# Three products of 256 columns in place of each one-element filler on TensorE, in the partial first and last passes of a pipelined block

## The chip, the cores and the metric

The kernel runs on one NeuronCore of a Trainium2 chip. The metric is the device time of one execution in microseconds. The other engines named here are VectorE (DVE), ScalarE (ACT), GpSimd (POOL) and SyncE (SP), which issues the transfers. TensorE is PE, and its weight loads are shown as PEld.

## The reference

Two gated cross-attention and feed-forward layers over 64 batch rows, each of 256 tokens by 256 features, with a context of 120 tokens. Cut to what matters:

```python
x = x + tanh(g_xattn[0]) * L0_xattn(ctx, ctx, layernorm(x))    # 16 heads, softmax over the heads
x = x + tanh(g_ffn[0])   * L0_ffn(layernorm(x))                # silu(x Wg) * (x Wu) Wd, hidden 768
x = x + tanh(g_xattn[1]) * L1_xattn(layernorm(x), ctx)         # 16 heads that share one key and value
x = x + tanh(g_ffn[1])   * L1_ffn(layernorm(x))                # x (W + low rank).T + b
```

## The kernel before, in words

The four parts are the stages A, B, C and D of a software pipeline. Pass t runs stage A of batch row t - 2, stage B of the row before it, stage C of the row before that, and stage D (with the second half of C) of the row three behind; `live(t, behind)` says whether such a row exists. With 64 rows the passes run from t = 2 to t = 68. The passes 5 to 65 are a hardware loop in which every stage is live. The three passes ahead of it (2, 3, 4) and the three behind it (66, 67, 68) are written out and are partial.

On each engine the order of a pass is written out by hand in `one_pass`, and the engines wait for one another through semaphores that count passes. So that the counts stay right in a partial pass, an operation whose row does not exist is replaced by a filler which raises the same semaphore: on TensorE `skipped(bank)` at L1217, a product of one element by one element into the bank that the real operation would write; on DVE a memset of one element (L842), on ACT a copy of one element (L516), on POOL a memset of one element (L361). The wait in front of the operation stands ahead of the filler too.

Names that the prediction uses, by the semaphore that TensorE raises. Stage A: T_mm_A (transposes, L1120), k0_mm (keys, L1098), q_mm_A (queries, 12 products, L1081 to L1083), A0_mm and A1_mm (scores of a half of the tokens, L1173), A0_sub and A1_sub (subtract the maximum, L1189), v0_mm (L1104). Stage B: yA1_mm (attended values, L1203), woA_mm (14 products), T_mm_B, G_mm 0 to 5 (12 products each), dn_mm 0 to 5. Stage C: T_mm_C, kv1_mm, q_mm_C, M0_mm and M1_mm (L1162), mT_mm (L1196), T0_mm and T1_mm (L1183), zC1_mm, woC_mm. Stage D: T_mm_D and f1_mm (14 products). `ln_A` to `ln_D` are the layer norms that ACT applies (L475), after DVE's moments (L775 to L784) and POOL's root (L336 and L339).

A product in float32 is two instructions of TensorE, one in float32r (`w_hi`, `w_lo`, the `xt_`, `y_` and `h_` tiles) is one.

Of the kernel before, what the change touches and what calls it, by code (L numbers as in the profile page):

```python
# [29 lines left out]
B, S, SC, D = 64, 256, 120, 256  # L30
H, HD = 16, 16
HID = 768
P = 128
# [44 lines left out]
def flamingo_kernel(nc, xp, cp, wc, wf, wi, brow, gates, cst, ldT, da, luT, uaT, out):  # L78
# [3 lines left out]
    with ctx:  # L82
        def sb(name, shape, dt=F32):
            return ctx.enter_context(nc.sbuf_tensor(name, shape, dt))
# [5 lines left out]
        w_hi = sb("w_hi", [P, WCOLS], F32R)  # L90
        w_lo = sb("w_lo", [P, WCOLS], F32R)
        ident = sb("ident", [P, P])
# [11 lines left out]
        key_bias = sb("key_bias", [P, 2, KC])  # L104
        bias_row = sb("bias_row", [1, 2 * D])
        val_bias = sb("val_bias", [P, D])
        spare = {e: sb(f"spare_{e}", [1, 400]) for e in ("act", "dve", "pool")}
        minus_half = sb("minus_half", [P, NT])

        x_ln = sb("x_ln", [P, NT, D])  # L110
# [941 lines left out]
        def _(pe):  # L1052
# [3 lines left out]
            for i, name in enumerate(("q0", "k0")):  # L1056
                for x in range(KC):
# [3 lines left out]
                      start=True, stop=True).then_inc(s["bias_mm"], 1)  # L1061
# [4 lines left out]
            for kc in range(KC):  # L1066
                last = pe.matmul(W[2][:, kc * D:(kc + 1) * D], t2_s[:, kc * P:(kc + 1) * P], uaT_s[:, :],
                                 start=True, stop=True)
# [146 lines left out]
                                lambda r, par: e1[0:SC, cc, r, par, :], 0, S)  # L1215

            def skipped(bank):  # L1217
                return pe.matmul(bank[0:1, 0:1], ident[0:1, 0:1], ident[0:1, 0:1], start=True, stop=True, skip_group_check=True)

            def one_pass(t):  # L1220

                pe.wait_ge(s["res_D"], t - 1)
                if live(t, 2):
                    gate_up(W[0], 5).then_inc(s["G_mm"], 1)
                else:
                    skipped(W[0]).then_inc(s["G_mm"], 1)
                pe.wait_ge(s["max_rows"], 64 * (t - 1))
                pe.wait_ge(s["A1_exp"], nth(0, 2, t))
                if live(t, 3):
                    scores1(0).then_inc(s["T0_mm"], 1)  # L1230
                else:
                    skipped(scores[:, 0, :]).then_inc(s["T0_mm"], 1)
                pe.wait_ge(s["v0_pad"], t - 1)
                if live(t, 2):
                    down(W[2], 0).then_inc(s["dn_mm"], 1)
                else:
                    skipped(W[2]).then_inc(s["dn_mm"], 1)
# [235 lines left out]
```

## Time and profile before

| | |
|---|---|
| time, median of 3 | 2813.01 us (2812.63 to 2813.55) |
| the profiled execution's own time | 2812.17 us |
| its span | 2810.4 us |
| PE busy | 2656.1 us (95%) |
| DVE busy | 2469.6 us (88%) |
| ACT, POOL busy | 1563.9 us (56%), 1427.9 us (51%) |
| mean granted TensorE clock | 0.987 |
| first filler of TensorE | 46.3 us |
| last filler of TensorE | 2807.4 us |

Times in the rows are counted from the span's start. The row PEclk gives the clock that TensorE was granted, 1.00 (2.4 GHz) or 0.50 (1.2 GHz); a mean between the two is a stretch with a change in it. "Idle before" is the time in which an engine had nothing running ahead of the group, and the name after it is what ended the wait.

### The profile page before, as it was taken

Reading aid. Unit: us, or ns where it says so; the run is one execution under the profiler, and the core shown is the slowest. Engines: PE = TensorE matmul, PEld = TensorE weight load, DVE = VectorE, ACT = ScalarE, POOL = GpSimd, SP = SyncE. Lnnn points to the kernel's source line nnn. Section 1 sums busy time; section 2 is a strip of 40 time slices with the busy share of each in tenths; the row PEclk is TensorE's granted clock in tenths of the full one; section 3 lists DMA queues with packets and bytes.
Section 4 is the critical chain, followed back from the end, with each engine's and each line's share of the span. In section 5 each row is a group of like instructions: output and inputs, shape, how many; then the busy total and the mean of one; then the engine's idle time right before and its main releaser. Section 6 shows DMA issues by size and latency. Waiting matters only on the chain.

```text
span 2810.4 us, 75822 instructions
## 1 busy us (share of the span) xinstructions
PE 2656.1 (95%) x30576; PEld 2278.9 (81%) x30576; DVE 2469.6 (88%) x4425; ACT 1563.9 (56%) x3125; POOL 1427.9 (51%) x1591
## 2 busy tenths in 40 slices
PE   3799999999999999999999999999999999999996
PEld 2688888888888888888888888888888888888884
DVE  4589999999999999999999999999999999999973
ACT  3355555555555555555555555555555555555553
POOL 1454465465455455456456446546545545545630
PEclk9799999999999999999999999999999999999997
DMA  2000000000000000000000000000000000000000
GB/s 76 24 22 25 26 25 29 23 27 28 21 28 27 21 30 25 21 30 25 25 27 25 25 26 27 28 21 27 28 21 30 25 21 30 25 21 30 25 16 9
DMA packets 74668, 73.15 MB, mean 26 GB/s; under 512 B 6907, under 2 KB 73745, under 8 KB 74642
## 3 DMA queue, kind: packets, MB, share of 16 engines
q1 hardware_dynamic: 74642, 72.80, 8.5%
q8 instruction: 17, 0.28, 0.0%
q14 instruction: 9, 0.07, 0.0%
HBM read 54.94 MB, written 16.78 MB: 26 GB/s over the span
## 4 chain that ended last, share of the span: by engine, by line
PE 36%; DVE 25%; POOL 24%; issue 6%; ACT 3%; DMA 2%; SPq 2%; POOLq 1%; DVEq 0%
POOL zt L345 8%; PE work L1081 8%; POOL h_lo L342 8%; PE work L1203 7%; PE work L1083 6%; PE work L1082 6%; DVE m L821 5%; POOL zt L349 4%; PE scores L1173 3%; DVE x L836 3%; POOL zt L352 2%; DVE y1f L833 2%; DVE e L830 2%; ACT e L509 2%; DMA x_ln<-xp 2%
## 5 line engine op out<-in xcount | busy, mean ns | idle before, releaser
L509 ACT ACTIVATE e<-scores 120x1024 f32<-120x1024 f32 x512 | 504.6, 1024 | 178.7 <-PE scores L1183 163.8
L342 POOL TENSOR_TENSOR h_lo<-h_f,h_hi 128x256 fp32r<-128x256 f32 x384 | 401.9, 1061 | 192.4 <-ACT h_hi L468 192.4
L1081 PE MATMUL work<-xt_hi_B,w_hi 128*128 128x256 f32 x1536 | 442.4, 288 | 0.9 <-DVE h_f L811 0.5
L1082 PE MATMUL work<-xt_lo_B,w_hi 128*128 128x256 f32 x1536 | 429.4, 280 | 0.0
L1083 PE MATMUL work<-xt_hi_B,w_lo 128*128 128x256 f32 x1536 | 428.5, 279 | 0.0
L830 DVE TENSOR_TENSOR e<-e,rz 120x2048 f32<-120x2048 f32 x128 | 383.8, 2998 | 2.2
L345 POOL TENSOR_TENSOR zt<-e 120x512 f32<-120x512 f32 x256 | 332.0, 1307 | 57.4 <-ACT e L509 57.4
L817 DVE TENSOR_REDUCE m<-scores 120x128 fp32r<-120x2048 f32 x128 | 293.3, 2291 | 27.6 <-PE scores L1173 24.3
L1081 PEld LDWEIGHTS work<-xt_hi_B,w_hi 128*128 128x128 f32 x1536 | 289.1, 188 | 11.8 <-DVE h_f L811 0.7
L1082 PEld LDWEIGHTS work<-xt_lo_B,w_hi 128*128 128x128 f32 x1536 | 289.5, 188 | 2.9
L1083 PEld LDWEIGHTS work<-xt_hi_B,w_lo 128*128 128x128 f32 x1536 | 289.1, 188 | 0.0
L336 POOL TENSOR_TENSOR rstd_B<-var_eps_B,minus_half 128x2 f32<-128x2 f32 x64 | 67.2, 1050 | 425.0 <-DVE var_eps_B L784 425.0
L336 POOL TENSOR_TENSOR rstd_D<-var_eps_D,minus_half 128x2 f32<-128x2 f32 x64 | 44.1, 689 | 463.3 <-DVE var_eps_D L784 463.3
L821 DVE TENSOR_REDUCE m<-scores 128x16 f32<-128x1920 f32 x128 | 274.8, 2147 | 5.0 <-PE scores L1162 4.8
L1081 PE MATMUL work<-w_hi,h_hi 128*128 128x256 f32 x768 | 228.9, 298 | 30.1 <-POOL h_lo L342 30.1
L1203 PE MATMUL work<-e,v_pad 120*32 120x128 f32 (+1 forms) x6144 | 237.7, 311 | 1.1 <-DVE e L830 1.1
L468 ACT ACTIVATE h_hi<-h_f 128x256 fp32r<-128x256 f32 x384 | 148.0, 420 | 142.2 <-DVE h_f L811 142.1
L833 DVE RECIPROCAL y1f<-y1f 128x256 f32<-128x256 f32 x128 | 222.8, 1742 | 2.0 <-ACT y1f L568 2.0
L1203 PEld LDWEIGHTS work<-e,v_pad 120*32 120x32 f32 x6144 | 180.2, 111 | 45.8 <-DVE e L830 1.6
L1082 PE MATMUL work<-w_lo,h_hi 128*128 128x256 f32 x768 | 214.8, 280 | 0.0
L1083 PE MATMUL work<-w_hi,h_lo 128*128 128x256 f32 x768 | 214.8, 280 | 0.0
L1081 PEld LDWEIGHTS work<-w_hi,h_hi 128*128 128x128 f32 x768 | 144.3, 188 | 81.4 <-POOL h_lo L342 60.1
(192 smaller groups left out, 7323.1 us busy)
## 6 DMA issues: line engine op xcount, KB each, us to landing
x_ln<-xp SPq DMA_DIRECT2D x64, 256.0 KB, 2.7
x_res<-xp SPq DMA_DIRECT2D x64, 256.0 KB, 2.7
y<-y_out SPq DMA_DIRECT2D x64, 256.0 KB, 2.2
ctx_f_A<-cp SPq DMA_DIRECT2D x64, 128.0 KB, 2.5
ctx_f_C<-cp SPq DMA_DIRECT2D x64, 128.0 KB, 2.0
qm<-mT SPq DMA_DIRECT2D x256, 4.0 KB
e<-wi SPq DMA_DIRECT2D x3, 768.0 KB, 5.9
e<-wf SPq DMA_DIRECT2D x2, 512.0 KB, 3.6
```

The lines of the kernel that those rows point to most:

```text
L342: return pool.tensor_tensor(h_lo[:, m, :], h_f[:, m % 2, :], h_hi[:, m, :].bitcast(F32), ALU.subtract)
L345: return pool.tensor_tensor(zt[0:SC, c, 4 * h:4 * h + 4, :], e0[0:SC, c, 2 * h, :, :], e0[0:SC, c, 2 * h + 1, :, :], ALU.add)
L468: return act.activation(out, src, ACT.Copy)
L509: return act.activation(e[0:SC, c, 2 * h:2 * h + 2, :, :].rearrange("p a b n -> p (a b n)"), scores[0:SC, 2 * h:2 * h + 2, :].rearrange("p ...
L817: return dve.tensor_reduce(m0[0:SC, c, :], scores[0:SC, :, :].rearrange("p r (h n) -> p n (r h)", n=P), AX.X, ALU.max)
L821: return dve.tensor_reduce(m1[:, c, :].rearrange("p (r x) -> p r x", r=RG)[:, :, 0:4], scores[:, :, :].rearrange("p r (h n) -> p r h n", n ...
L830: return dve.tensor_tensor(e, e, rz0[0:SC, c:c + 1, :].to_broadcast([SC, H, P]), ALU.mult)
L833: return dve.reciprocal(y1f[:, cc * S:(cc + 1) * S], y1f[:, cc * S:(cc + 1) * S])
L1081: pe.matmul(out, a_hi, b_hi_, start=first, stop=False, skip_group_check=parts)
L1082: pe.matmul(out, a_hi, b_lo_, start=False, stop=False, skip_group_check=parts)
L1083: last = pe.matmul(out, a_lo, b_hi_, start=False, stop=end, skip_group_check=parts)
L1203: last = pe.matmul(bank[32 * r:32 * r + 32, cc * S + query:cc * S + query + n], v_of(4 * cc + r, par), e_of(r, par), start=par == 0, stop= ...
```

## The change

Each filler of TensorE becomes three products in float32r of 128 by 128 by 256: weights `w_hi[:, 0:128]`, moving data `w_hi[:, 0:256]`, written over the first 256 columns of the same bank on all its 128 partitions. Only the last raises the semaphore. The fillers of the other engines stay, and the spare tiles that they write are cut from 400 to 170 elements.

```diff
-        spare = {e: sb(f"spare_{e}", [1, 400]) for e in ("act", "dve", "pool")}
+        spare = {e: sb(f"spare_{e}", [1, 170]) for e in ("act", "dve", "pool")}
...
             def skipped(bank):
-                return pe.matmul(bank[0:1, 0:1], ident[0:1, 0:1], ident[0:1, 0:1], start=True, stop=True, skip_group_check=True)
+                for n in range(3):
+                    last = pe.matmul(bank[:, 0:S], w_hi[:, 0:P], w_hi[:, 0:S], start=True, stop=True, skip_group_check=True)
+                return last
```

TensorE at the start of pass 2, from its first filler to the keys of stage A; `work` is one of the four banks, `scores` the first bank of the scores:

```order
-L1218 MATMUL work<-ident 1x1
-L1218 MATMUL scores<-ident 1x1
-L1218 MATMUL work<-ident 1x1 x4
-L1218 MATMUL scores<-ident 1x1
-L1218 MATMUL work<-ident 1x1 x8
+L1219 MATMUL work<-w_hi 128x256 x3
+L1219 MATMUL scores<-w_hi 128x256 x3
+L1219 MATMUL work<-w_hi 128x256 x12
+L1219 MATMUL scores<-w_hi 128x256 x3
+L1219 MATMUL work<-w_hi 128x256 x24
 L1120 MATMUL work<-ident,xn_A 128x128 x4
 L1098 MATMUL work<-ctx_f_A,wk 128x128 x4
```

The same fifteen fillers stand in the same places, now as 45 products; nothing changes place.

TensorE in pass 68, the last, from the first scores of stage C to the last attended values:

```order
 L1183 MATMUL scores<-qm,km 128x256 x8
-L1218 MATMUL work<-ident 1x1 x4
+L1219 MATMUL work<-w_hi 128x256 x12
 L1183 MATMUL scores<-qm,km 128x256 x8
 L1203 MATMUL work<-e,ones_pad 32x256 x8
-L1218 MATMUL work<-ident 1x1 x2
+L1219 MATMUL work<-w_hi 128x256 x6
 L1203 MATMUL work<-e,ones_pad 32x256 x8
-L1218 MATMUL work<-ident 1x1
+L1219 MATMUL work<-w_hi 128x256 x3
 L1203 MATMUL work<-e,v_pad 32x256 x16
```

Twelve products stand between the two score groups instead of four one-element fillers, and six between the two sums over the keys.

## Rows read from the trace of the kernel before

**Rows 1.** The page: TensorE's share, and two rows of the 40 equal slices.

```profile
PE 2656.1 (95%) x30576; PEld 2278.9 (81%) x30576; DVE 2469.6 (88%) x4425; ACT 1563.9 (56%) x3125; POOL 1427.9 (51%) x1591
...
PE   3799999999999999999999999999999999999996
...
PEclk9799999999999999999999999999999999999997
```

**Rows 2.** Windows: stretch, length, PE, PEld, DVE, ACT, POOL busy, clock, DMA.

```profile
51.40:58.80 7.40, 6.13 (x36) 5.46 (x34) 1.69 (x11) 1.87 (x7) 0.18 (x2) 1.00 0.14 37
59.50:62.90 3.40, 1.34 (x36) 1.14 (x36) 1.88 (x2) 0.58 (x4) 0.00 (x0) 1.00 0.02 5
63.40:74.50 11.10, 8.80 (x56) 5.72 (x57) 5.86 (x12) 4.79 (x12) 6.04 (x9) 0.56 0.13 36
...
94.40:100.80 6.40, 6.17 (x30) 5.73 (x30) 1.43 (x6) 2.06 (x5) 0.09 (x1) 0.53 0.00 0
...
2749.20:2752.60 3.40, 1.72 (x15) 1.35 (x14) 3.18 (x6) 2.06 (x7) 0.00 (x0) 1.00 0.00 0
2752.60:2759.40 6.80, 5.79 (x38) 4.66 (x37) 2.80 (x6) 1.97 (x6) 0.09 (x1) 0.50 0.01 2
2761.40:2767.00 5.60, 0.61 (x14) 0.31 (x10) 3.43 (x11) 1.38 (x5) 0.89 (x2) 0.94 0.00 0
...
2801.00:2807.00 6.00, 4.65 (x27) 4.02 (x28) 0.94 (x7) 1.28 (x9) 0.35 (x4) 0.50 0.01 3
```

**Rows 3.** TensorE's fillers by form: count, ns min/median/max, first and last start.

```profile
L1218 PE MATMUL work<-ident x162: 158/158/160, 46.3 to 2807.4; 1*1 1x1 f32 x162
...
L1218 PE MATMUL scores<-ident x60: 158/158/160, 46.5 to 2807.1; 1*1 1x1 f32 x60
```

**Rows 4.** Timeline of passes 2 and 3: start, length, engine, line; pairs of successive products.

```profile
57.14 0.41 PE L1083 MATMUL work<-xt_hi_A,w_lo 128*128 128x256 f32 x1
...
57.35 0.41 PE L1081 MATMUL work<-xt_hi_A,w_hi 128*128 128x256 f32 x1
...
103.09 0.28 PE L1083 MATMUL work<-xt_hi_B,w_lo 128*128 128x256 f32 x1
...
103.20 0.28 PE L1081 MATMUL work<-xt_hi_B,w_hi 128*128 128x256 f32 x1
```

**Rows 5.** Timeline of pass 2 and the start of pass 3.

```profile
46.57 0.46 PE L1218 MATMUL work<-ident 1*1 1x1 f32 x8
...
49.38 1.09 ACT L475 ACTIVATE xn_A<-x_ln,shift_A,rstd_A 128x256 f32<-128x256 f32 x2 [0.52 <-POOL shift_A L339]
...
51.42 1.11 PE L1120 MATMUL work<-ident,xn_A 128*128 128x128 f32 x4
...
52.32 1.91 PE L1098 MATMUL work<-ctx_f_A,wk 128*128 128x128 f32 x8
...
66.68 2.09 PE L1173 MATMUL scores<-qt_A,kz 32*128 32x128 f32 x32 [1.01 <-ACT e L509]
...
68.82 2.07 PE L1104 MATMUL work<-w_ctx,ctx_f_A 128*128 128x256 f32 x4
68.84 2.29 DVE L817 TENSOR_REDUCE m<-scores 120x128 fp32r<-120x2048 f32 x1 [2.03 <-PE scores L1173]
...
80.10 1.94 PE L1203 MATMUL work<-e,v_pad 120*32 120x128 f32 x32
...
83.17 1.93 PE L1203 MATMUL work<-e,v_pad 120*32 120x128 f32 x32 [1.14 <-DVE e L830]
```

**Rows 6.** Timeline of pass 3: the same transposes, keys and scores.

```profile
90.02 0.74 PE L1120 MATMUL work<-ident,xn_A 128*128 128x128 f32 x4
...
90.92 1.13 PE L1098 MATMUL work<-ctx_f_A,wk 128*128 128x128 f32 x8 [0.16 <-DVE x L836]
...
107.70 1.17 PE L1173 MATMUL scores<-qt_A,kz 32*128 32x128 f32 x32
```

**Rows 7.** Timeline of pass 68: TensorE's scores, and ACT behind them.

```profile
2781.73 2.09 PE L1183 MATMUL scores<-qm,km 32*128 32x256 f32 x16 [1.96 <-ACT e L509]
...
2783.89 1.94 ACT L509 ACTIVATE e<-scores 120x1024 f32<-120x1024 f32 x2 [2.03 <-PE scores L1183]
```

## The prediction

> **What bounds the kernel now.** I read the page's slices first. TensorE is busy 95% of the span, and only the first two slices and the last show less [rows 1]. The granted clock is low in the same places, so whatever this change does, it does in about 110 us at the start and about 60 us at the end; the loop between them holds no filler. Next I read windows by stage. In a partial pass the chain goes from engine to engine: TensorE waits for DVE, POOL or ACT, and what it does next often runs at 1.2 GHz. From 63.4 to 74.5 us the mean clock is 0.56, from 94.4 to 100.8 it is 0.53, from 2752.6 to 2759.4 and from 2801 to 2807 it is 0.50 [rows 2]. The clock fell behind stretches in which TensorE had little to do: 1.34 us busy of 3.40 ahead of 63 us, 1.72 of 3.40 ahead of 2752.6, 0.61 of 5.60 ahead of 2767 [rows 2].
>
> One row has to be read with care. Between 51.4 and 58.8 us the clock is shown as 1.00 [rows 2], but the products there start 0.21 us apart, against 0.11 to 0.12 us at 103 us [rows 4]. TensorE was at 1.2 GHz there too; I go by the distance of products. The Trainium skill, "TensorE: Matmul & The Clock Gate", Part 1, "Seeing it yourself", warns that single clock events in a trace have been unreliable. By that sentence the trace agrees; my sums use product distances in any case.
>
> **The change part by part.** Removed are 162 + 60 = 222 instructions [rows 3]. One float32 filler is two of them, so there are 111 fillers. Eight instructions in a row took 0.46 us [rows 5], so a filler costs about 0.1 us of TensorE. Added are 333 products of 128 by 256. The nearest rows are kernel products of the same shape: 0.115 us apart at 2.4 GHz, 0.213 at 1.2 [rows 4]. A new filler then costs 0.35 or 0.64 us, +0.25 or +0.54 over the old. As a link in a chain of waits its last product ends some 0.28 + 2 x 0.115 = 0.5 us after its start instead of 0.16 [rows 3, 4]. All of them: 111 x 0.25 = 28 us more PE time at 2.4 GHz, 60 at 1.2. Most of it lies in waits that exist now; what doesn't is paid. What is bought is clock: 0.098 us per product of 256 columns that stood at 1.2 GHz, 0.92 per score group (2.09 against 1.17), 0.8 for the keys (1.91 against 1.13), 0.4 for the transposes (1.11 against 0.74) [rows 4 to 6].
>
> The cut of the spare tiles moves addresses and no work: 0.
>
> Stage by stage along the chain, in us (minus is faster), each with its ends:
>
> 1. Pass 2 up to the queries. ACT may apply ln_A only after the zC1 filler, and ten fillers, 30 products, stand up to there from 46.3 us. At 1.2 GHz they take 6.4 us and end at 52.7; if the clock rises after fourteen, 14 x 0.213 + 16 x 0.115 = 4.8 us and 51.1. Now ln_A starts at 49.4 [rows 5]: +1.7 to +3.4, I take +2.4. Three more fillers stand between ln_A and the transposes, partly in waits: +0.9. Behind them TensorE has been busy long enough to be at full clock: transposes -0.4, keys -0.8, twelve query products -1.2. Sum +0.9; ends 0 and +4.7.
> 2. Rest of pass 2. DVE's maximum (2.29 us) leaves TensorE idle, two fillers fill 0.7 of it, and I expect the clock to fall as now. Then f1 filler, v0 (2.07 at half clock) and mT filler are 0.64 + 2.07 + 0.64 = 3.35 us behind a maximum of 2.29 [rows 5]: +1.0; one subtraction may still find full clock, -0.5. Sum +0.5; ends -1.9 and +1.0.
> 3. Pass 3, attended values. POOL's sums of the heads leave TensorE idle for four us. Then dn4, dn5 and zC1 fillers (1.9 at half clock) stand ahead of 1.94 us of work that had 3.1 us until the second half could start at 83.17 [rows 5]: +0.3, ends -0.5 and +0.6. But TensorE is then busy without a break, and woA (14 products) should find full clock: 14 x 0.098 = -1.4, I take -1.1.
> 4. Pass 3, queries and first gate: 24 products between 94.4 and 100.8 us, 24 x 0.098 = -2.4 if two more fillers in the idle stretch ahead hold the clock, 0 if not. I take -0.9.
> 5. Pass 4: six fillers, T0 and T1 behind POOL's work, the others in dense TensorE work. With the T_D filler of pass 3: +1.0.
> 6. Pass 66: ten fillers; the two A0_sub ones stand straight ahead of the stage D transposes, four others in dense work or under DVE's maximum: +0.6, ends 0.3 and 0.9.
> 7. Pass 67, q_mm_C to M1_mm. The clock fell after 1.72 us busy of 3.40; yA1 and woA fillers lift that by some 0.5. If it holds: twelve products -1.2 and one score group -0.9, a little being covered, -2.0. If not, T_A and k0 fillers at 0.64 stand ahead of M0: +0.7. I take -0.6. Stage D of this pass comes after 5.6 us with 0.61 busy [rows 2]; seven fillers make that about 3.0, spread out: 0.
> 8. Pass 68, T0 to zC1. At full clock two score groups gain 0.9 each and the sum over the keys 0.4. At half clock the four dn fillers (2.56 us) outlast ACT's 1.94 us of exponentials [rows 7], and dn4, dn5 add again: +0.6 and +1.2. Mixed: -0.4; ends -2.2 and +1.8. woC: seven fillers under 4 us of DVE work, 12 products -1.3 or +0.6: -0.1.
> 9. Pass 68, stage D. T_B to A0_sub are nine fillers close together ahead of the transposes and f1, which stand at 0.50 now [rows 2]. Full clock: -0.4 and 14 x 0.098 = -1.4. I take -1.1; ends -1.8 and +0.9.
>
> Sum: +0.9 + 0.5 + 0.3 - 1.1 - 0.9 + 1.0 + 0.6 - 0.6 - 0.4 - 0.1 - 1.1 = -0.9 us. The profiled execution took 2812.17 us (span 2810.4 and 1.8 around it), so 2811.3; the median of the runs lies 0.8 above it, which gives 2812.1, said as 2812.
>
> **The rivals.**
> A, full clock nearly throughout. For it: the fillers put work into every gap, and the clock fell on narrow margins (1.72 of 3.40). The Trainium skill, same page, Part 1, "What's actually happening", says that the clock is held back by default and that activity releases it; by that rule the fillers' products keep it released. From rows: 0.2 - 1.9 - 0.5 - 1.4 - 2.4 + 1.0 + 0.3 - 2.0 - 2.2 - 1.3 - 1.8 = -12.0, and up to -1.8 more in stage D of pass 67: about 2800. Against it: three products fill 0.35 us, the gaps under DVE's maxima (2.3) and POOL's sums (4 us) are longer.
> B, slower, one mechanism: fillers at half clock stand in TensorE's queue ahead of work that is ready. It decides when the clock does not rise on the first thirty products at 46.3 us and falls at every wait. The upper ends: 4.7 + 1.0 + 0.6 + 1.0 + 0.9 + 0.7 + 1.8 + 0.6 + 0.9 = +12.2: 2825. For it: the waits that are there now are of other engines, and at 0.64 us a filler two of them outlast many. Against: dense products have raised the clock wherever they ran, as between 94.4 and 100.8.
> C, the change does not do what it says: the clock rises and falls where it does now, most fillers are hidden, those at half clock are paid: items 1, 3, 5, 6 and 7 at 0.9 + 0.3 + 1.0 + 0.6 + 0.7 = +3.5, the others 0: 2816.5.
>
> **How the numbers follow.** Forecast (gains and costs about even) 0.55, its own range 2807.5 to 2816.5; A 0.17; B 0.10; C 0.18. The range of 8 in 10 reaches from 2804.5, half-way into A, to 2818. A measurement of this kernel can tell about 0.2% (5.6 us) from no change. Faster by more: nearly all of A and little else, 0.19; slower by more: B and a bit of C, 0.12; within: 0.69.
>
> **What would show it.** The profile after should have 333 products of L1219 at about 280 ns at full and 415 ns at half clock. ln_A should start near 51.8 us instead of 49.4 (item 1), the queries' products 0.115 us apart. The windows after each of DVE's maxima in pass 2 should show 0.50 still (item 2), woA of pass 3 1.00 (item 3). In the last pass f1 should be at full clock (item 9). The loop should start within 3 us of where it does, its 61 passes unchanged. I am wrong if the mean clock of the first 110 us comes near 1.00 (A), if it stays at 0.5 over the first fillers and ln_A starts after 53 us (B), or if the passes of the loop change their length, for which I see no reason in the rows.

## The result, and the profile after

The changed kernel takes 2803.56 us (median of 8 runs, 2801.67 to 2807.07), the kernel before on the same chips 2812.61 (8 runs, 2809.33 to 2813.55). The ratio is 0.9971, 95% interval 0.9960 to 0.9982: 9 us faster by the medians (8 by the ratio, which is not their plain quotient), where 0.9 was forecast, and just below the range. The profiled execution is the slowest of the eight, 2807.07 us with a span of 2805.0. Set against the profile of before (2810.4) it shows 5.4 us of the 9.

The page after: TensorE's share, and the same two rows of 40 slices as in [rows 1].

```profile
PE 2673.7 (95%) x30687; PEld 2303.5 (82%) x30687; DVE 2468.7 (88%) x4425; ACT 1567.0 (56%) x3125; POOL 1430.1 (51%) x1591
...
PE   3899999999999999999999999999999999999998
...
PEclk9899999999999999999999999999999999999999
```

TensorE is busy 18 us longer in a shorter span. The clock in the last slice is now 9 where it was 7, and in the second slice 8 where it was 7.

Windows of the kernel after, for [rows 2]: stretch, length, PE, PEld, DVE, ACT, POOL busy, clock, DMA. The first four are the same stretches; the others are moved so that they hold the same work.

```profile
51.40:58.80 7.40, 6.60 (x49) 6.19 (x47) 1.55 (x14) 3.97 (x16) 0.18 (x2) 1.00 0.12 37
59.50:62.90 3.40, 2.73 (x47) 2.56 (x46) 0.06 (x1) 1.01 (x4) 0.00 (x0) 1.00 0.00 0
63.40:74.50 11.10, 8.85 (x68) 7.31 (x66) 6.55 (x15) 4.13 (x12) 5.14 (x9) 0.85 0.05 17
94.40:100.80 6.40, 5.42 (x31) 5.21 (x31) 1.35 (x6) 2.62 (x7) 0.09 (x1) 0.73 0.01 3
2751.60:2755.00 3.40, 2.34 (x20) 2.10 (x20) 3.18 (x6) 2.05 (x8) 0.00 (x0) 1.00 0.00 0
2755.00:2761.80 6.80, 5.95 (x63) 4.84 (x61) 4.00 (x8) 2.14 (x7) 0.09 (x1) 1.00 0.00 0
2763.80:2769.40 5.60, 3.63 (x25) 3.07 (x25) 2.21 (x16) 2.59 (x10) 1.16 (x5) 1.00 0.01 3
2777.40:2787.40 10.00, 9.13 (x117) 5.89 (x117) 1.96 (x9) 5.10 (x11) 0.30 (x4) 1.00 0.01 2
2795.80:2801.80 6.00, 4.65 (x38) 4.27 (x38) 1.10 (x7) 2.42 (x11) 0.83 (x6) 1.00 0.00 0
```

The stretch in which TensorE was busy 1.72 of 3.40 us now has 2.34, and the clock stays at 1.00 through the queries and key scores behind it, which stood at 0.50. The stretch with 0.61 of 5.60 now has 3.63. The last layer norm and its products stood at 0.50 and stand at 1.00.

The timeline after, for [rows 5 to 7]: start, length, engine, line.

```profile
48.05 2.76 PE L1219 MATMUL work<-w_hi 128*128 128x256 f32 x12
...
53.28 1.07 ACT L475 ACTIVATE xn_A<-x_ln,shift_A,rstd_A 128x256 f32<-128x256 f32 x2
...
56.52 1.06 PE L1098 MATMUL work<-ctx_f_A,wk 128*128 128x128 f32 x8
...
61.96 1.17 PE L1173 MATMUL scores<-qt_A,kz 32*128 32x128 f32 x32 [0.67 <-ACT qt_A L484]
...
68.30 1.86 PE L1173 MATMUL scores<-qt_A,kz 32*128 32x128 f32 x32
...
2780.89 1.15 PE L1183 MATMUL scores<-qm,km 32*128 32x256 f32 x16 [0.60 <-ACT e L509]
...
2801.63 0.69 DVE L836 TENSOR_TENSOR y_out<-work,x 128x512 f32<-128x512 f32 x1 [2.02 <-PE work L1086]
```

Twelve of the first thirty filler products take 2.76 us, which is one every 0.21 us: half clock, although the clock row still reads 1.00 there. ln_A starts 3.9 us later than in [rows 5]; the keys take 1.06 us instead of 1.91. The second score group of pass 68 takes 1.15 us instead of 2.09 [rows 7]. The last residual (`y_out`), which started at 2806.99 us before, starts 5.4 us earlier.

### The profile page after: what moved, and what is told of

It is laid out like the page before. It is cut to its first block, busy times and chain, and to the rows that moved or that the text cites. A ratio compares the mean times of both kernels' runs of the same rounds, so it can differ in the third digit from the quotient of the medians.

```text
span 2805.0 us, 76044 instructions
## 1 busy us (share of the span) xinstructions
PE 2673.7 (95%) x30687; PEld 2303.5 (82%) x30687; DVE 2468.7 (88%) x4425; ACT 1567.0 (56%) x3125; POOL 1430.1 (51%) x1591
## 4 chain that ended last, share of the span: by engine, by line
PE 40%; POOL 33%; DVE 17%; issue 4%; ACT 3%; POOLq 1%; SPq 0%; DMA 0%; DVEq 0%
POOL zt L345 12%; POOL h_lo L342 11%; PE work L1203 10%; PE work L1081 8%; PE work L1082 7%; PE work L1083 7%; POOL zt L349 6%; DVE m L821 5%; POOL zt L352 3%; DVE x L836 3%; PE scores L1173 3%; ACT e L509 3%; DVE kz L794 2%; PE work L1110 1%; PE work L1120 1%
```

## The experiments

Each ran in five rounds beside the kernel before. A ratio is that of a kernel's times to those of the kernel before in the same rounds, with its 95% interval; it can differ a little from the quotient of the medians. The edits are to `skipped`; `p` is the pass (written out, so a number) and `k` the filler's number in it. Each short diff is against the changed kernel.

**Which end.**

```diff
-                for n in range(3):
+                for n in range(3 if p < 10 else 0):   # e1; 0 is the old one-element filler
```

> Three products per filler in passes 2 to 4 only, the old one-element fillers in passes 66 to 68. My theory now: the gain of 9 us is made at the end, where the clock stays at full from pass 66 on, and the front comes out even, because the first thirty filler products cost about 4 us before ln_A starts (53.3 us instead of 49.4) and the clock then gives them back. Expected: within 1.5 us of the kernel before (2811 to 2814), loop starting within 1 us of before. The rival, that both ends gain in proportion to the time spent at half clock (some 55 us of it in front, some 40 at the end), expects 2807 to 2809.

Measured: 2810.92 us (11 runs), ratio 0.9995 (0.9986 to 1.0004). By the interval it is not told from the kernel before, as the theory said. The details came out a little faster than expected: the median is just below the range of 2811 to 2814, and in the profile, with ln_A at 52.94 us, the first maximum over the heads behind pass 4 starts 1.8 us earlier than before (141.95 against 143.72), where within 1 us was expected.

```diff
-                for n in range(3):
+                for n in range(0 if p < 10 else 3):   # e2
```

> The reverse: three products per filler in passes 66 to 68 only. My theory: nearly the whole change, 2803 to 2805, with the mean clock of the last 60 us at 0.95 or more. The rival of equal shares expects 2808.

Measured: 2806.06 us (9 runs), ratio 0.9974 (0.9964 to 0.9984). Most of the change is made at the end, against 2812.48 for the kernel before in the same rounds: 6.4 us here and 1.6 in e1, 8.0 together of the 9. It came out 1 us short of what I expected. Windows of its end, with the columns as above:

```profile
2745.00:2760.00 15.00, 13.48 (x151) 10.10 (x143) 9.47 (x19) 7.13 (x17) 1.81 (x6) 1.00 0.01 1
2760.00:2775.00 15.00, 9.87 (x81) 8.33 (x79) 6.32 (x25) 4.41 (x19) 1.53 (x10) 1.00 0.05 18
2775.00:2790.00 15.00, 13.19 (x133) 9.24 (x134) 4.60 (x16) 5.99 (x15) 0.39 (x5) 0.89 0.01 2
2790.00:2804.00 14.00, 11.24 (x85) 10.07 (x83) 4.47 (x24) 4.04 (x21) 1.24 (x6) 1.00 0.06 20
```

The clock is the last column but two: one short drop (0.89) in 59 us. The kernel before, in stretches of 15 us:

```profile
2750.00:2765.00 15.00, 9.53 (x81) 7.41 (x82) 9.95 (x22) 3.82 (x14) 0.17 (x2) 0.77 0.00 1
2765.00:2780.00 15.00, 8.02 (x62) 5.97 (x62) 1.69 (x11) 4.01 (x17) 1.45 (x10) 0.66 0.05 19
2780.00:2795.00 15.00, 9.94 (x106) 5.41 (x107) 5.29 (x18) 5.87 (x18) 0.38 (x5) 0.73 0.01 2
```

**The same time on TensorE with less of the array.**

```diff
-                    last = pe.matmul(bank[:, 0:S], w_hi[:, 0:P], w_hi[:, 0:S], ...)
+                    last = pe.matmul(bank[0:1, 0:S], w_hi[0:1, 0:1], w_hi[0:1, 0:S], ...)   # e3
```

> Three products of 256 columns everywhere as in the changed kernel, but of one weight row and one weight column (1 by 1 by 256): the same time on TensorE, nearly none of the array in use. If the clock follows how long TensorE is busy, the result is that of the changed kernel, 2803 to 2805, full clock at the end. If it follows how much of the array works, the clock falls where it fell before and the fillers are pure cost: 2814 to 2818.

Measured: 2823.43 us (5 runs), ratio 1.0037 (1.0023 to 1.0050). It is slower than the kernel before by 11 us, more than expected. A stretch of pass 2, its end, and one pair of its products in pass 2:

```profile
70.00:85.00 15.00, 15.00 (x79) 8.36 (x79) 8.56 (x22) 5.39 (x16) 9.31 (x11) 0.50 0.09 28
...
2765.00:2780.00 15.00, 11.33 (x92) 6.84 (x90) 8.10 (x24) 5.17 (x21) 1.42 (x8) 0.86 0.01 1
2780.00:2795.00 15.00, 13.97 (x79) 8.75 (x83) 1.12 (x11) 3.45 (x11) 0.42 (x6) 0.50 0.05 19
2795.00:2810.00 15.00, 14.01 (x116) 7.77 (x109) 6.36 (x17) 4.15 (x13) 0.18 (x2) 0.73 0.01 2
```

```profile
63.34 0.41 PE L1083 MATMUL work<-xt_hi_A,w_lo 128*128 128x256 f32 x1
63.56 0.41 PE L1081 MATMUL work<-xt_hi_A,w_hi 128*128 128x256 f32 x1
```

TensorE, with the thin fillers in its gaps, is busy 15.00 and 13.97 us of 15.00 and has the clock 0.50. The queries of pass 2 start 0.21 us apart, as in [rows 4] before: half clock. Ahead of them TensorE was busy for 15.22 of 15.40 us (46.7 to 62.1), mostly with thin products. So the fillers' time on TensorE gains nothing by itself: the changed kernel's gain comes with the clock, and the thin kernel shows what fillers cost without it.

```diff
+                    last = pe.matmul(bank[0:1, 0:S], w_hi[:, 0:1], w_hi[:, 0:S], ...)   # e12: 128 rows, one column
```

> Three products of 256 columns with all 128 weight rows and one weight column (128 by 1 by 256). With one row and one column the clock fell (2823.4). If what counts is the data that moves through the array's rows, this holds the clock: 2803 to 2805. If it is the cells in use, it is 2820 or more. I think the cells: 2820.

Measured: 2805.42 us (9 runs), ratio 0.9973 (0.9963 to 0.9982). My guess was wrong: with one column on 128 rows the end of the kernel ran at 0.89 and more, near the changed kernel's.

```profile
2775.00:2790.00 15.00, 12.65 (x135) 6.62 (x135) 4.69 (x17) 6.05 (x17) 0.38 (x5) 0.89 0.01 2
2790.00:2805.00 15.00, 12.11 (x83) 8.66 (x81) 4.37 (x24) 3.79 (x19) 1.24 (x6) 0.89 0.05 18
```

```diff
+                    last = pe.matmul(bank[:, 0:S], w_hi[0:1, 0:P], w_hi[0:1, 0:S], ...)   # e15: one row, 128 columns
```

> Three products with one weight row and all 128 columns (1 by 128 by 256). One row and one column let the clock fall (2823.4), 128 rows and one column held it (2805.4). If the rows that data moves in on are what counts, this is as slow as the thin one: 2820 to 2825. If any extent of the array will do, 2803 to 2807.

Measured: 2826.47 us (5 runs), ratio 1.0054 (1.0040 to 1.0068). With one row on 128 columns the same stretches ran at 0.61.

```profile
2775.00:2790.00 15.00, 12.95 (x81) 11.35 (x80) 1.84 (x13) 4.18 (x15) 0.60 (x8) 0.61 0.05 19
2790.00:2805.00 15.00, 14.90 (x108) 8.71 (x101) 5.04 (x12) 4.33 (x12) 0.18 (x2) 0.61 0.01 2
```

Among these fillers the number of rows, which weights and moving data share, told the fast kernels from the slow ones; the number of columns did not. Only 1 and 128 rows were run, nothing between.

**The moved addresses alone.**

```diff
-                for n in range(3):
+                for n in range(0):   # e4: the old filler, spare tiles of 170 elements
```

> The old one-element fillers with the spare tiles cut to 170 elements: the part of the change that moves addresses only. My theory: nothing, within 1 us of the kernel before. The rival, that part of the 9 us is from the moved addresses (the two profiles differ by 2 us over the 61 passes of the loop, which the fillers don't touch), expects a difference of 2 us or more and another length of the loop.

Measured: 2812.13 us (11 runs), ratio 0.9998 (0.9989 to 1.0007). Nothing. From the first maximum behind pass 4 to the same one before pass 66 its profile has 2543.07 us, the kernel before 2542.06, the changed one 2544.08, e1 2543.12: over all seventeen profiles it lies between 2542.06 and 2544.96. The 2 us between the two profiles' loops are no more than one profile differs from another, and with the medians alike (e4) nothing shows them to be an effect of the change.

**How many products.**

```diff
-                for n in range(3):
+                for n in range(1):   # e5; 2 in e11, 6 in e6
```

> One full product of 256 columns per filler instead of three. If the narrow margins of item 7 are what counts (the clock fell with TensorE 1.72 of 3.40 us busy), one product adds too little in the idle stretches at the end: the clock falls there in some places, between the kernel before and the changed one, about 2808, and the front costs less. If any activity of the full array holds the clock, it should equal or beat the changed kernel: 2801 to 2803.

> Two products per filler. One gave 2810.4, three 2803.6, six 2813.8. If the gain comes in steps, place by place as the clock holds, two lies between one and three: 2804 to 2808. If the queue's cost is already large at three, two is the best: 2801 to 2803.

> Six products per filler. The clock should never fall in the partial passes, but at 0.69 us per filler at full clock the queue itself is the chain: pass 68 has 31 fillers, nine of them between woC and the stage D transposes, 6.2 us where the chain has 4.4. My theory: slower than the changed kernel by some 5 us or more, 2808 to 2814, clock 0.999. The rival, that only the clock counts and the fillers stay hidden, expects 2800 to 2803.

Measured: one 2810.42 us, ratio 0.9996 (0.9987 to 1.0005); two 2804.76, 0.9974 (0.9963 to 0.9984); six 2813.75, 1.0011 (1.0002 to 1.0020). One is worth nothing that can be told, where about 2808 was expected. Two is not told from three. With six the mean clock is 0.999 or 1.000 in every run, and the kernel is slightly slower than before, inside the range expected for it. Pass 68 of the kernel with six, windows and the fillers ahead of the last layer norm's transposes:

```profile
2775.00:2790.00 15.00, 14.20 (x161) 10.93 (x160) 2.29 (x11) 5.90 (x15) 0.51 (x7) 1.00 0.06 20
2790.00:2805.00 15.00, 15.00 (x128) 14.85 (x124) 6.04 (x26) 4.81 (x21) 1.33 (x7) 1.00 0.01 2
```

```profile
2800.77 1.09 ACT L475 ACTIVATE xn_D<-x,shift_D,rstd_D 128x256 f32<-128x256 f32 x2 [0.81 <-POOL shift_D L339]
2801.72 1.60 PE L1226 MATMUL scores<-w_hi 128*128 128x256 f32 x12
...
2803.16 0.60 PE L1120 MATMUL work<-ident,xn_D 128*128 128x128 f32 x4
```

ACT has ln_D done at 2801.9 us, and the transposes start 1.3 us later, behind twelve filler products. TensorE, busy 15.00 of 15.00, is now what the others wait for here. This is the mechanism of rival B, at full clock.

**The head of pass 2.**

```diff
-                for n in range(3):
+                for n in range(0 if p == 2 and k < 10 else 3):   # e7
```

> The changed kernel with the first ten fillers of pass 2 (up to zC1, which ACT waits for before ln_A) left at one element. Item 1 of the prediction: ln_A starts at 49.4 us instead of 53.3, but transposes, keys and queries are at half clock again. The prediction's sizes (+2.4 + 0.9 against -2.4) say +0.9 for the whole, so this should be 1 us faster or less, 2802 to 2803.5. A rival: the early products are what puts the clock up for the rest of pass 2, without them it is slower by 2 us: 2805 to 2806.

Measured: 2801.97 us (6 runs), ratio 0.9965 (0.9953 to 0.9977). The direction is as expected, and the rival's 2805 to 2806 did not come, but the interval overlaps the changed kernel's, so it is not shown to be faster. ln_A starts at 50.11 us in its profile.

```diff
+            for n in range(16):   # e8, ahead of the last waits of the setup
+                pe.matmul(W[0][:, 0:S], w_hi[:, 0:P], w_hi[:, 0:S], ...)
```

> The changed kernel plus sixteen products of the same kind at the end of the setup, when TensorE waits for DVE's memset (from about 39 to 46.6 us, the weights being ready at some 43). They lie in that wait, 16 x 0.213 = 3.4 us. My theory: the clock is up at the first filler, the thirty products take 3.5 us instead of some 6, ln_A starts near 50.5 instead of 53.3: 2 to 3 us faster, 2800.5 to 2801.5. The rival, that the front is bounded by POOL's sums and the time is lost again by pass 3, expects no change, 2803 to 2804.

Measured: 2803.36 us (7 runs), ratio 0.9972 (0.9961 to 0.9983): no change against the changed kernel. ln_A starts at 52.11 us, 1.2 us earlier than after and not 2.8. The premise failed: the clock was not up at the first fillers, for the same twelve products take the same 2.76 us.

```profile
41.61 3.78 PE L1072 MATMUL work<-w_hi 128*128 128x256 f32 x16 [2.69 <-DVE w_lo L766]
...
47.62 2.76 PE L1228 MATMUL work<-w_hi 128*128 128x256 f32 x12
```

The rival's figure was right; that POOL's sums are what takes the time back was not tested.

**The end, pass by pass.**

```diff
-                for n in range(3):
+                for n in range(3 if p == 68 else 0):   # e9; p == 67 in e14, p >= 67 in e13
```

> Three products per filler in pass 68 only. The chains of the two profiles say that pass 68 gave 5.5 us (scores and sum over the keys 2.3, woC 1.3, stage D 1.9) and pass 67 some 2.3. So my theory expects 5.5 us of the 6.4 that both end passes gave: 2806 to 2808, pass 67 with its drop of the clock as before. A rival: pass 68 starts at full clock only because pass 67 ended so; alone it would bring half of that, 2809 to 2810.

> Three products per filler in passes 67 and 68. All three end passes gave 6.4 us, pass 68 alone 3.2. If the fillers of pass 67 let pass 68 begin at full clock, this is the whole of the 6.4: 2805 to 2806.5. If the fillers of pass 66 hold something too, it stays at 2807 to 2808.

> Three products per filler in pass 67 only. If the two passes add up, this gives the difference of 3.2 us: 2809. If pass 67's products are worth something only with those of pass 68, it gives less: 2810.5 to 2812. The chain of the changed kernel puts 1.9 us on pass 67's queries and key scores, which need no help from pass 68, so I expect 2 us: 2810.5.

Measured: pass 68 alone 2809.30 us, ratio 0.9989 (0.9980 to 0.9998); pass 67 alone 2808.74, 0.9992 (0.9983 to 1.0001); both 2805.87, 0.9979 (0.9970 to 0.9988). In medians against the kernel before in the same rounds: 3.2, 3.0 and 5.9 us. By its interval pass 67 alone is not told from the kernel before. In the medians the two passes add up, and both together gave what was expected of them; pass 68 alone gave less than the 5.5 us expected, pass 67 alone more than the 2. Pass 66 is worth nothing that shows (6.4 with it). Why pass 68 alone gave 3.2 is seen in its windows and its two score groups:

```profile
2755.00:2770.00 15.00, 7.27 (x83) 5.37 (x81) 8.21 (x25) 5.08 (x19) 1.24 (x6) 0.77 0.00 1
2770.00:2785.00 15.00, 11.64 (x87) 9.20 (x87) 1.33 (x13) 3.88 (x15) 0.59 (x8) 0.66 0.06 20
2785.00:2800.00 15.00, 13.39 (x126) 10.12 (x119) 7.20 (x26) 5.63 (x21) 1.06 (x4) 1.00 0.00 1
```

```profile
2777.99 2.09 PE L1183 MATMUL scores<-qm,km 32*128 32x256 f32 x16 [2.73 <-DMA qm<-mT]
...
2782.87 1.46 PE L1183 MATMUL scores<-qm,km 32*128 32x256 f32 x16
```

From 2770 to 2785 us it still ran at a mean of 0.66, as before; the clock was up from 2785 on. With fillers in pass 67 alone (e14) it is the other way round: the first score group of pass 68 is at full clock, the second at half.

```profile
2776.59 1.15 PE L1183 MATMUL scores<-qm,km 32*128 32x256 f32 x16 [2.64 <-DMA qm<-mT]
...
2779.96 2.09 PE L1183 MATMUL scores<-qm,km 32*128 32x256 f32 x16 [1.96 <-ACT e L509]
```

So part of what I had put to pass 68, from one pair of profiles, is bought by the fillers of pass 67.

**Three products only where needed.**

```diff
-                for n in range(3):
+                for n in range(0 if (p == 2 and k < 10) or p == 66 or (p == 4 and k > 2) else 3):   # e10
```

> The changed kernel with three products only where the clock needs them: left at one element are the first ten fillers of pass 2, the last three of pass 4 (dense work around them) and all ten of pass 66, where the clock never fell. My theory: up to 1 us better than the kernel with the bare head alone (2801.97), about 2801. The rival, that the fillers of pass 66 and of the end of pass 4 are hidden, expects the same 2802.

Measured: 2803.14 us (6 runs), ratio 0.9969 (0.9957 to 0.9981). By the interval it is not told from e7: leaving out the fillers of pass 66 and of the end of pass 4 changes nothing that shows, which is what the rival said. No version was shown to be faster than the changed kernel.

## Why the prediction was wrong

It was right that the time would change at the ends, that the clock was what could be bought and fillers in the queue what it costs, and that the spare tiles do nothing (e4). The front was nearly right in its sum, but by luck: the errors of its items, up to 1.7 us, cancel. Read from the two chains (after minus before, each step from the one before it):

- Item 1, said +0.9: ln_A 3.9 us later, the first scores 2.1 us later, of which 0.3 is a later start of the fillers. So +1.8. The low end had the clock rise after fourteen products; in the profile the first twenty-one took 4.6 us, from 46.63 to 51.25, at half clock, and ln_A came later than even the high end of +3.4.
- Item 2, said +0.5: -1.2. I expected the clock to fall behind the maximum and stay down; the mean was 0.85 between 63.4 and 74.5 us, not 0.56.
- Items 3 and 4, said +0.3 - 1.1 - 0.9: +1.1, -1.5 and -0.5.
- Item 5, said +1.0: +0.3. The front, with the later start, comes to +0.4 in this pair of profiles where +0.7 was said; e1's medians have a gain of 1.6 us there, which its interval does not tell from none.

**The step that failed is the sizing of items 7 to 9**, the mixtures at the end. The mechanisms stood there with their ends; I put the terms near the middle. Item 7, said -0.6 and 0 for its stage D: -1.9 and -0.45. Item 8, said -0.4 and -0.1 for woC: -2.3 and -1.3, both at their lower ends. Item 9, said -1.1: -1.9. Item 6 was +0.1, said +0.6. The end together was said to be -1.6; the pair of profiles has -7.8, and e2 measures 6.4 us over nine runs. Nearly all of the miss is there. What the runs showed in place of the middle is full clock: each of these terms but stage D of pass 67 came out within 0.1 us of what its item gave for a clock that holds.

Behind it is how I read the busy share. I took each short stretch alone, asked whether the clock could fall somewhere in it, and counted a doubt as half a loss. The cases hung together more than that: with fillers in pass 67 alone, the first score group of pass 68 was at full clock too (1.15 us against 2.09). In the profile after, the clock fell once in the last 60 us, in stage D of pass 67, where I had counted on no gain. There TensorE had been busy 3.63 of 5.60 us, more than the 3.0 that I had worked out, and the clock fell all the same. Why it held in all the other gaps at once is not isolated.

Two of the signs misled. ln_A started at 53.28 us, past the 53 that was to speak for B, and the time still came out near A, because the front decides little of it. And that dense products "have raised the clock wherever they ran" was too much to say against B: before, the fourteen products that end pass 68 stood in a stretch at 0.50 [rows 2].

Rival A gave 2800 for full clock nearly throughout; the measured 2803.6 is its mechanism without the front's share. A's terms for the end add up to -7.0, and the profiles have -7.8; its terms for the front add up to -5.0, and the profiles have +0.4. The Trainium skill's sentence cited there ("TensorE: Matmul & The Clock Gate", Part 1, "What's actually happening") says that activity releases the clock. Our runs agree for products on 128 rows (e12, 2805.4 us) and disagree if any product is meant: with the thin ones TensorE was busy 15.00 of 15.00 us at the clock 0.50 (e3). Rival B had the price right in kind: e3 is +10.9 us and e15 +14.7, where 12.2 was worked out. Between the full fillers and the thin ones lie 20 us.

The range was also too narrow for a kernel whose executions differ so. The profiled execution alone, 2807.1, lies inside it, but the median doesn't. In that execution the clock fell in pass 4, and in the profiles of e1, e7 and e8 it did not. From 115 to 130 us, first after, then e1:

```profile
115.00:130.00 15.00, 11.46 (x121) 10.58 (x119) 9.10 (x24) 4.39 (x14) 11.25 (x12) 0.77 0.00 1
```

```profile
115.00:130.00 15.00, 9.65 (x129) 8.94 (x128) 8.69 (x23) 5.72 (x19) 10.34 (x12) 1.00 0.04 10
```

Nothing in the order differs there, nor in pass 2, where from 60 to 70 us the mean clock is 0.83 after and 1.00 in e1. The kernel's own executions reach over 5.4 us, and their mean clocks go the same way: 0.996 or 0.997 in the four slowest (2804.0 to 2807.1 us), 0.998 or 0.999 in the four fastest (2801.7 to 2803.1). That this spread is the clock falling at different places is likely from this, but was not isolated; in e13, which has the old fillers in front, the slowest run (2808.08 us) has the highest mean clock (0.997).

## What to carry to other kernels

Where TensorE waits on a chain through other engines, look at the clock of the work behind the wait: here the wait cost a second time, as half clock. Products on all 128 rows in the wait bought that back, as long as they were not longer than the wait. How many matters on both sides: one product per filler bought nothing that shows, two and three about 8 to 9 us, and with six the queue ate the gain. Price the clock by what a whole stretch of the program would do at either level, with both ends kept in the range, and don't average doubts gap by gap.

## What the runs showed of the hardware

In this kernel, three filler products of 1 x 1 x 256 or 1 x 128 x 256 (rows by columns of weights, by columns of moving data) gave 2823.4 and 2826.5 us, and three of 128 x 1 x 256 or 128 x 128 x 256 gave 2805.4 and 2803.6. From 2775 to 2790 and from 2790 to 2805 us the mean clock was 0.52 and 0.73, 0.61 and 0.61, 0.89 and 0.89, and 1.00 and 1.00, in this order.

The clock row of the profile read 1.00 at the start also where products start 0.21 us apart, as from 51.4 to 58.8 us before and from 62 to 64.6 us in e3; their distance tells the level. Products of 128 by 128 by 256 in float32r, each with its own weights, start 0.115 us apart at full clock and 0.213 at half [rows 4].
